# First seven units of a fused attention and quantized feed-forward kernel in another order, with idle products and a later rounding of the ffn weights

## The reference

```
x = L0_attn_x                                     # (16, 256, 256)
q, k, v = (layernorm(x) @ w.T for w in (wq, wk, wv))
scores = q @ k.T / sqrt(128), masked: (k <= q) & ((k < 4) | (k >= q - 31))
x = x + (softmax(scores) @ v) @ wo.T
w_q = round(weight / (max|weight| / 127));  x_q = round(n / (max|n| / 127)),  n = layernorm(x)
x = x + (x_q @ w_q.T) * x_scale * w_scale + bias
```

## Time and profile before

| | before |
|---|---|
| median of 3 runs | 606.07 us (605.48 to 607.39) |
| profiled execution, its own time | 607.0 us |
| its span (first to last instruction) | 605.1 us |
| PE busy | 593.6 us, 98% |
| DVE busy | 536.3 us, 89% |
| ACT busy | 401.0 us, 66% |
| POOL busy | 313.6 us, 52% |
| mean granted TensorE clock | 0.989 |

### The profile page before, as it was taken

How to read it: one execution, slowest core, us unless ns; L and a number is a source line. 1 busy time by engine, 2 the same in 40 slices (tenths; PEclk the granted TensorE clock), 3 DMA queues, 4 the chain that set the end, 5 groups by cost and what they waited for, 6 DMA issues and landing times.

```text
span 605.1 us, 18063 instructions
## 1 busy us (share of the span) xinstructions
PE 593.6 (98%) x7556; PEld 524.7 (87%) x7556; DVE 536.3 (89%) x1072; ACT 401.0 (66%) x633; POOL 313.6 (52%) x310
## 2 busy tenths in 40 slices
PE   8999999999999999999999999999999999999995
PEld 7779888898988989888898988989898898988983
DVE  7899999898988979899898989979899898879987
ACT  7898665676666666666667566567666666666673
POOL 2155364555646455564646647455564645646473
PEclk8899999999999999999999999999999999999997
DMA  8748042150604316060250604216060330505001
GB/s 305 236 89 192 2 110 51 61 116 19 159 15 94 69 38 140 19 134 25 72 105 20 157 19 105 56 42 135 20 140 2 92 68 36 125 19 121 21 3 52
DMA packets 36272, 49.69 MB, mean 82 GB/s; under 512 B 2784, under 2 KB 22240, under 8 KB 36192
## 3 DMA queue, kind: packets, MB, share of 16 engines
q1 hardware_dynamic: 36048, 48.41, 32.6%
q10 hardware_dynamic: 144, 0.13, 0.1%
HBM read 35.42 MB, written 12.58 MB: 79 GB/s over the span
## 4 chain that ended last, share of the span: by engine, by line
PE 92%; DVE 5%; ACT 1%; issue 1%; DMA 0%; POOL 0%; DVEq 0%; POOLq 0%
PE ps L416 27%; PE ps L538 26%; PE ps L447 8%; PE ps L395 7%; PE ps L384 6%; PE ps L491 5%; PE ps L521 5%; PE ps L520 5%; PE ps L372 1%; PE ps L584 1%; PE ps L553 1%; DVE Qs L1070 1%; PE ps L569 1%; DVE pool L1097 0%; DMA X<-in_L_attn_x 0%
## 5 line engine op out<-in xcount | busy, mean ns | idle before, releaser
L416 PE MATMUL ps<-xT,WqT 128*128 128x256 f16 x1536 | 181.6, 275 | 1.0 <-DVE Qs L1070 0.7
L538 PE MATMUL ps<-WoT,pool 128*128 128x256 f16 x1440 | 167.3, 273 | 0.2 <-DVE pool L1097 0.2
L416 PEld LDWEIGHTS ps<-xT,WqT 128*128 128x128 f16 x1536 | 148.3, 99 | 18.6 <-DVE Qs L1070 1.0
L538 PEld LDWEIGHTS ps<-WoT,pool 128*128 128x128 f16 x1440 | 138.4, 98 | 15.4 <-DVE pool L1097 0.3
L1504 POOL TENSOR_TENSOR small<-E,rr 128x576 f32<-128x576 f32 x64 | 73.7, 1152 | 109.5 <-DVE rr L1092 109.3
L892 ACT ACTIVATE pool<-ps 128x512 f16<-128x512 f32 x128 | 70.2, 594 | 82.0 <-PE ps L521 82.0
L818 ACT ACTIVATE Qs<-ps 128x576 f16<-128x576 f32 x128 | 82.7, 646 | 43.7 <-PE ps L416 43.7
L1510 POOL TENSOR_TENSOR PP<-small,PP 128x576 f16<-128x576 f32 x64 | 82.0, 1282 | 52.6 <-ACT PP L879 52.6
L1070 DVE TENSOR_TENSOR Qs<-ps,Qs 128x576 f16<-128x576 f32 x128 | 92.8, 728 | 4.0 <-ACT Qs L818 4.0
L1493 POOL TENSOR_TENSOR Sm<-Sm,mx 128x576 f32<-128x576 f32 x64 | 73.7, 1152 | 36.1 <-DVE mx L1083 34.7
L1097 DVE SCALAR_TENSOR_TENSOR pool<-ps,pool 128x512 f16<-128x512 f32 x128 | 82.3, 681 | 0.2
(11 more groups left out here) (134 smaller groups left out, 893.5 us busy)
## 6 DMA issues: line engine op xcount, KB each, us to landing
values<-Vn SPq DMA_DIRECT2D x32, 256.0 KB, 2.0
VW<-values SPq DMA_DIRECT2D x16, 480.0 KB
big<-values SPq DMA_DIRECT2D x16, 480.0 KB
X<-in_L_attn_x SPq DMA_DIRECT2D x16, 256.0 KB, 8.4
VW<-values SPq DMA_DIRECT2D x16, 240.0 KB
big<-values SPq DMA_DIRECT2D x16, 240.0 KB
out<-pool SPq DMA_DIRECT2D x15, 256.0 KB, 6.0
big<-in_L_attn_wq SPq DMA_DIRECT2D x4, 512.0 KB, 8.0
```

The costliest lines, as they stand in the source:

```text
L416: a = pe.matmul(banks[BANK_Q[f]][:, j * 256:j * 256 + 256], WqT[:, k, wl, h * 128:h * 128 + 128], xT[:, b % 2, k, xl, :], start=(n == 1), ...
L538: a = pe.matmul(out_view(b, t), OT[:, p, ol, h, t * 128:t * 128 + 128], WoT[:, 4 * g + h, wl, :], start=first, stop=(end and g == KV - 1), ...
```

## The change

1. **The order of units 0 to 6** is written anew on PE, ACT, DVE and POOL. The queries of the next unit stand before and between the scores, layer-norm pieces move, and the first `x_evac` on DVE now stands behind `scale("q0")` and `ln_stats(1)`.
2. **Shared scales**: the tiles q2 and q3 go through one `scale_sums` and one `scale`, each two columns wide. `scale_sums("q3")` and `scale("q3")` are gone, and of four `exp_scale` operations two are left, of one and of three columns.
3. **Idle products**: two before `scale_sums("q0")`, one before `scale_sums("v")`, three before `k_fill(0, 0)`.
4. **The ffn weights**: `ffn_weight_scale` goes from unit 4 to the end of the list by hand, and `ffn_weight_round` into the eighth unit (t == 7) of the loop.

```
-        SUMS_ORDER = ("k", "q0", "v", "q1", "q2", "q3", "o")
+        SUMS_ORDER = ("k", "q0", "v", "q1", "q2", "o")
+        def scale_of(name):
+            return "o" if name[0] == "o" else "q2" if name == "q3" else name
+        def n_columns(name):
+            return 2 if name == "q2" else 1
...
+            def idle_products(n):
+                for _ in range(n):
+                    pe.matmul(banks[BANK_S[0]][:, 0:128], small_ones[:, :], small_ones[:, :], start=True, stop=True)
...
             x_transpose(0)
+            idle_products(2)
             scale_sums("q0")
+            idle_products(1)
             scale_sums("v")
+            idle_products(3)
             pe.wait_ge(xt_ok, 1)
...
             weight_low("k", (1,))
-            x_evac(0)
             scale("q0")
             ln_stats(1)
-            exp_scale(0)
+            x_evac(0)
             scale("v")
...
-            ffn_weight_scale()
...
-            ffn_weight_round()
...
             v_low(2, 1)
+            ffn_weight_scale()
...
                     ffn_peak(norm)
+                if t == FIRST:
+                    ffn_weight_round()
```

More of the change, by code:

```diff
@@ L356, in scale_sums @@
                     pe.wait_ge(v_l, 2)
[L357 to L360, removed]
+                n, w = KV if name == "o" else 1, n_columns(name)
+                pe.wait_ge(w_am[name], n * w)
+                for i in range(n):
+                    c = SCALES[name] + i
+                    a = pe.matmul(all_sums(name), small_ones[:, :], am[:, c:c + w], start=(i == 0), stop=(i == n - 1))
                 a.then_inc(w_all[name], 1)
@@ L648, in _ @@
             q_fill(2, 0)
+            x_transpose(1)
             q_fill(2, 1)
[L650 to L654, removed]
             pe.wait_ge(xt_ok, 2)
@@ L658, in _ @@
             k_fill(1, 0)
+            q_fill(3, 0)
+            p_transpose(0)
+            q_fill(3, 1)
             scores(2)
+            pe.wait_ge(k_l, 3)
+            v_fill(1, 0)
             q_fill(4, 0)
+            scale_sums("o")
             pv(0, 0)
             pv(0, 1)
[L664 to L665 removed]
             pe.wait_ge(s_m, 3)
@@ L675, in _ @@
             q_fill(5, 0)
+            q_fill(5, 1)
+            x_transpose(2)
             pv(1, 0)
             pv(1, 1)
-            x_transpose(2)
-            q_fill(5, 1)
             p_transpose(2)
@@ L1305, in _ @@
             weight_low("v")
+            ln_norm(1)
+            weight_low("q1")
+            q_low(0, 0)
             k_low(0, 0)
-            q_low(0, 0)
             q_low(0, 1)
-            weight_low("q1")
             v_low(0, 0)
-            ln_norm(1)
+            v_low(0, 1)
+            exp_scale(0, 1)
+            s_mask(0)
+            s_peak(0)
             scale("q2")
-            s_mask(0)
-            v_low(0, 1)
-            s_peak(0)
-            scale("q3")
             q_low(1, 0)
@@ L1319, in _ @@
             weight_low("q2")
-            weight_low("q3")
             probs(0)
             s_mask(1)
+            k_low(0, 1)
+            weight_low("q3")
             q_low(2, 0)
+            exp_scale(1, KV)
             s_peak(1)
@@ L1326, in _ @@
             ln_stats(2)
-            scale("o")
-            k_low(0, 1)
-            exp_scale(1)
-            q_low(3, 0)
-            weight_low("o0")
-            probs(1)
-            k_low(1, 0)
-            exp_scale(2)
-            ln_norm(2)
-            s_mask(2)
+            k_low(1, 0)
+            ln_norm(2)
+            q_low(3, 0)
+            probs(1)
+            s_mask(2)
+            s_peak(2)
+            scale("o")
             q_low(3, 1)
-            s_peak(2)
             q_low(4, 0)
@@ L1341, in _ @@
             v_low(1, 1)
-            o_low(0, 0)
+            weight_low("o0")
             probs(2)
-            o_low(0, 1)
             q_low(4, 1)
             s_mask(3)
-            exp_scale(3)
+            o_low(0, 0)
+            o_low(0, 1)
             s_peak(3)
-            ln_stats(3)
             k_low(1, 1)
@@ L1352, in _ @@
             probs(3)
+            q_low(5, 0)
             o_low(1, 0)
@@ L1355, in _ @@
             s_mask(4)
-            q_low(5, 0)
+            ln_stats(3)
             s_peak(4)
@@ L1366, in _ @@
             s_peak(5)
-            q_low(6, 0)
             q_low(6, 1)
```

140 lines of the change are left out of this document (70 added, 70 removed).

## The result

| | before | changed |
|---|---|---|
| median | 605.48 us (604.83 to 607.39, 15 runs) | 607.67 us (606.66 to 608.81, 15 runs) |
| profiled execution, its own time | 607.0 us | 606.69 us |
| its span | 605.1 us | 604.8 us |
| mean granted clock in it | 0.989 | 0.995 |
| `k_fill(0, 0)` starts | 11.01 us | 12.57 us |

The account below looks back on a forecast made before the run. PE, busy 98% of the span, was taken to bound the kernel. From the profiled 607.0 us, +0.17 (entry), -2.33 (clock), -0.14 (scales), -0.43 (waits) and +0.55 (rounding) gave 604.8 us, range 603.6 to 607.3.

Parts of the forecast that it names:

- The base: Starting point of the sum: the one profiled execution, 607.0 us, 0.93 above the median of the three runs.
- the clock term: At the start, idle products keep PE's clock up, so 24 `q_fill` matmuls take 2.62 us, not 4.95: -2.33 us.
- Shared scales: PE loses the q3 sum, the second column costs nothing, DVE loses some 0.6 us of operations: -0.14 us.
- The waits in units 0 to 3: PE's three early waits for DVE shrink from 2.17 to 1.74 us in the new order: -0.43 us.
- the placement: Profiled durations put in the new order, each instruction starting once engine and semaphores are free; gave the early waits, 1.74 us.
- Rounding in unit 8: Five more DVE operations ahead of `s_mask(8)` delay `q_low(9, 0)`, for which PE waits: +0.55 us.
- its old place: Unit 6, where the rounding stood: PE was full there, so removing it gains nothing, 0.
- Entry: Start to first queries: the later copy of `xT` delays `k_fill(0, 0)` to 12.40 and the first `q_fill` to 13.93: +0.17 us.
- idle products: Six added products on PE before `k_fill(0, 0)` fit into its waits and cost 0.
- Rival 1: The clock at the start still falls, for half as long: 606.6 us, chance 0.16.
- Rival 2: The clock at the start falls as long as before, with `k_fill` wholly in the slow stretch: 608.1 us, chance 0.10.
- Rival 3: DVE's slack swallows the rounding in unit 8 and early waits lose another 0.15: 604.1 us, chance 0.16.

Follow-up runs that it names:

- e1: The kernel before, run again with no edit: 605.34 us, ratio 0.9999 to the kernel before.
- e5: The changed kernel with only the middle operation of the shared scale cut into two of one column: 606.23 us, ratio 1.0008 to the kernel before.
- e6: The changed kernel with only the three-column `exp_scale` cut into three of one column: 607.75 us, ratio 1.0027 to the kernel before.
- e2: The changed kernel with both the shared scale's middle operation and the three-column `exp_scale` cut into single columns: 605.44 us, ratio 1.0004 to the kernel before.
- e7: e2 with `ffn_weight_scale` and `ffn_weight_round` back at their old places: 604.98 us, ratio 0.9996 to the kernel before.
- e4: The changed kernel with `ffn_weight_scale` and `ffn_weight_round` back at their old places: 606.86 us, ratio 1.0029 to the kernel before.
- e12: The changed kernel, run again with no edit: 606.84 us, ratio 1.0027 to the kernel before.
- e18: The changed kernel, run once more with no edit, to see where its clock falls: 608.35 us.

## Why the prediction was wrong

**The base (the clock term, -2.33): failed.** The step was to make the sum against one profiled execution and to carry it over to the median. In the pair of profiled executions the 24 matmuls took 2.62 us for 4.95, as said. Of these 2.33 us only 545.71 - 543.63 = 2.08 reach `scores(60)` (first profile of before against e1): with a slow PE, DVE gets further, and the wait ahead of `scores(1)` was 0.79 us there and 1.04 in e1. But the prediction called a spread of 1.9 us over the three runs a possible sign of a moving slow stretch, and then took the stretch as given in the base. In e1 it wasn't there. A base with the chance of the stretch in it would have left the term near nothing for the median. With 605.3 to 605.5 as the base and the other terms unchanged (+0.15 in sum) the forecast would have been about 605.6.

**Shared scales ("I price the second column at nothing, between 0 and 0.01"): failed, and this is the loss.** The step looked at PE's product of two columns, where it was right, and saw on DVE only operations that go, 0.6 us of them. The two wide operations stall beside POOL for 1.0 us each, of which 0.92 and 0.61 reach `scores(60)` (e5, e6). Of this term -0.14 became +1.4.

**The waits in units 0 to 3 (-0.43): mechanism right, hidden by the stall.** Without the stalls (e2) the three waits sum to 0.88 + 0.61 + 0.43 = 1.92 us from start to start, where 1.74 was placed; e1 has 2.42 at the three old ones, so the gain is 0.50. In the changed kernel they are 2.87. The further wait at 34.60 is the stall of `exp_scale`; in e2 0.19 us are left there, ahead of `scores(2)`.

**Rounding in unit 8 (+0.55) and its old place (0): right mechanism, wrong sizes.** The wait is at `L627`, ended by `q_low`, as said; it is 0.82 us (0.87 in e2). The old places were priced at nothing, since PE was full there; in the new order they cost 0.77 up to `scores(8)` (e7 against e2), so the net cost is 0.22. What share the held L1271 of `ffn_weight_scale` has in the wait stays open: e4 and e7 move both operations together.

**The agreement of the sum is luck.** From the first `q_fill` to `scores(60)` e2 differs from e1 by 543.60 - 543.63 = -0.03 us, and the prediction's terms there sum to -0.14 - 0.43 + 0.55 = -0.02. But up to `scores(8)` e2 gained 1.02 where 0.57 was predicted, and unit 8 gave back 0.93 where 0.55 was predicted.

**Entry (+0.17) and idle products (0): held** in this profile, at +0.27 against e1; in other executions without a slow stretch the first `q_fill` starts at 13.91 to 14.45 us with the late copy, and at 13.69 to 13.76 in the kernel before. The products cost nothing in it: `k_fill` still waited 0.19 us for `xT` behind them. **Rival 1** (the slow stretch stays, half as long) came true in a part of the executions, as e12 and e18 show: 1.86 and 1.67 us where 1.7 to 1.9 was worked out. **Rival 2** (a full one, 608.1) was never caught in the changed kernel. **Rival 3** fell: DVE had nothing to swallow the rounding with. No rival had the stall.

The sum by the runs, up to `scores(60)` and without a slow stretch: entry +0.27, scale stall +0.92, `exp_scale` stall +0.61, the rest of the placement -0.03 = +1.77, measured 1.76. What the median of the first 15 runs (607.67) has above the profiled 606.69 comes from longer executions: 8 of the 15 had a span over 605.5 us, at a mean clock of 0.992 to 0.994. How often these come differs from run to run, 607.67 there and 606.84 in e12.

## What to carry to other kernels

Before merging small vector operations into one wider, look in the trace for the shortest and the median time of existing operations of that width: where these are far apart (169 and 864 ns here), look whether it ends with an instruction of GpSimd. Here single columns of one source (0.10 to 0.15 us each) were cheaper than one operation of two or three; one column with two sources was held all the same. And before pricing a slow stretch of the clock, ask how many executions have it: compare the profiled execution's own time with the median and the fastest run, and cost the change against an execution without it as well.

## What the hardware showed unexpectedly

An operation on 256 numbers (128x2) can hold DVE for 1.15 us, seven times the 0.17 of other 128x2 operations, while 128x1 at the same place takes 0.13 to 0.15. A product of two 128x1 tensors was held for 0.98 us. And a mean busy share didn't tell whether the clock would fall: with 1.94 us of PE work between 8.34 and 11.76 us it stayed up (e1), with 2.10 in the same stretch it fell, the same program both times.
